# Three attentions of a transformer kernel: units of three heads taken in pairs

## The reference, cut to what matters

```python
# first: head size 64, values 16 wide per head, positional scores added
content_score = einsum('bind,bjnd->bnij', q + r_w_bias * SCALE, k)
attn_prob = softmax(content_score + rel_shift(pos_score), axis=-1)
attn_vec = einsum('bnij,bjnd->bind', attn_prob, v) @ Wo + bo
# second: head size 16, values 16 wide
# third:  head size 64, values 64 wide
scores = einsum('bqhd,bkhd->bhqk', q, k) * scale
out = einsum('bhqk,bkhd->bqhd', softmax(scores, axis=-1), v) @ Wproj
```

## Time and profile before

| | us |
|---|---|
| runs | 1655.21, 1665.26, 1647.38 (median 1655.21) |
| the profiled execution | 1649.25 |
| its span, first to last instruction | 1647.5 |
| PE busy / PEld / DVE / ACT / POOL | 1426.8 / 1050.3 / 684.2 / 664.3 / 387.5 |
| score matmuls L1928, 1152 records, busy | 140.8 |
| transposes L1967 / values L1957, busy | 92.7 / 85.9 |
| exponentials L1619 and accumulator reads, busy | 332.1 |
| key copies L1764 (48) and L1792, L1793 (48), busy | 28.4 and 24.2 |

### The profile page before, as it was taken

The page is one execution under the profiler, slowest core; times in us unless marked ns, Lnnn a source line. Parts: engine busy times, 40 slices in busy tenths (PEclk is TensorE's granted clock), DMA queues, the critical chain, the costliest instruction groups (busy, mean ns, idle before and its releaser), DMA issues.

```text
span 1647.5 us, 31617 instructions
## 1 busy us (share of the span) xinstructions
PE 1426.8 (87%) x10268; PEld 1050.3 (64%) x10268; DVE 684.2 (42%) x2126; ACT 664.3 (40%) x2241; POOL 387.5 (24%) x468
## 2 busy tenths in 40 slices
PE   5899897788779678888998998799999999989994
PEld 3556665643334456666678898376676776879993
DVE  5567766611112765444326322344343323451113
ACT  1668665320001337777531122265455442213331
POOL 5213212300000232222101565122121100024441
PEclk9899997578877799999999899799999999889997
DMA  7433432649997000000005664200000300135553
GB/s 224 125 100 103 115 90 56 235 161 418 419 417 226 5 0 1 0 0 0 0 0 144 184 198 123 61 2 0 0 0 0 134 0 0 41 118 183 184 164 106
DMA packets 94439, 178.73 MB, mean 108 GB/s; under 512 B 35578, under 2 KB 54168, under 8 KB 92704
## 3 DMA queue, kind: packets, MB, share of 16 engines
q1 hardware_dynamic: 80144, 130.65, 25.2%
q10 hardware_dynamic: 7056, 30.67, 4.5%
q0 software_dynamic: 7136, 16.10, 3.2%
HBM read 150.39 MB, written 26.99 MB: 108 GB/s over the span
## 4 chain that ended last, share of the span: by engine, by line
PE 61%; issue 12%; DVE 12%; ACT 6%; DMA 6%; SPq 2%; POOL 1%; DVEq 0%; ACTq 0%; POOLq 0%
PE bank L1837 15%; PE bank L2357 6%; PE bank L2343 5%; PE bank L1928 4%; DMA AREA<-in_fc 4%; PE bank L1940 4%; PE bank L1957 3%; PE bank L2347 3%; PE bank L1967 3%; PE bank L2018 2%; PE bank L1903 2%; ACT ON L1619 2%; PE bank L2010 2%; PE bank L2274 1%; DVE MXU L929 1%
## 5 line engine op out<-in xcount | busy, mean ns | idle before, releaser
L1837 PE MATMUL bank<-XT,AREA 96*128 96x408 f32 (+1 forms) x640 | 239.4, 532 | 33.1 <-ACT XT L1573 15.7
L1837 PEld LDWEIGHTS bank<-XT,AREA 96*128 96x128 f32 (+1 forms) x640 | 121.9, 196 | 139.7 <-issue 100.1
L1928 PE MATMUL bank<-KZ,QT 128*102 128x102 f32 x1152 | 140.8, 262 | 9.0 <-ACT PB L1619 5.8
L666 POOL TENSOR_TENSOR PB<-PB,RCU 102x306 f32<-102x306 f32 x96 | 69.2, 720 | 317.0 <-DVE RCU L935 316.9
L650 POOL TENSOR_TENSOR RS<-VE,expo 102x4 f32<-102x4 f32 (+1 forms) x53 | 53.0, 1000 | 376.0 <-DVE VE L875 326.3
L1928 PEld LDWEIGHTS bank<-KZ,QT 128*102 128x102 f32 x1152 | 122.4, 174 | 27.2 <-issue 18.2
L2357 PE MATMUL bank<-WM,KZ 128*128 x660 | 118.2, 327 | 0.0
L2357 PEld LDWEIGHTS bank<-WM,KZ 128*128 128x128 f32 x660 | 105.7, 190 | 0.4
L1600 ACT ACTIVATE KZ<-bank,AREA 128x128 f32<-128x128 f32 x198 | 54.8, 375 | 121.7 <-PE bank L2347 121.7
L1940 PE MATMUL bank<-AREA,OT 128*102 128x192 f32 x384 | 88.9, 345 | 11.3 <-DVE SLOTS L1291 5.2
L1957 PE MATMUL bank<-PT,V 102*32 102x102 f32 (+1 forms) x1152 | 85.9, 270 | 14.5 <-DVE OT L945 12.3
(11 more groups left out here) (335 smaller groups left out, 2734.3 us busy)
## 6 DMA issues: line engine op xcount, KB each, us to landing
AREA<-in_fc SPq DMA_DIRECT2D x10, 1536.0 KB, 21.5
SLOTS<-in_m3w SPq DMA_DIRECT2D x33, 384.0 KB
WM<-in_fc ACTq DMA_DIRECT2D x5, 2304.0 KB, 14.5
WM<-in_fc SPq DMA_DIRECT2D x6, 1536.0 KB, 21.2
AREA<-in_fc ACTq DMA_DIRECT2D x4, 2304.0 KB, 15.2
SLOTS<-in_m1w SPq DMA_DIRECT2D x33, 256.0 KB
AREA<-pos_scratch SPq DMA_DIRECT2D x16, 459.0 KB
pos_scratch<-AREA SPq DMA_DIRECT2D x8, 913.5 KB
```

Of the source, the lines that this page charges most:

```text
L666: pool.tensor_tensor(p, p, scale, ALU.mult).then_inc(sem["probs_ready"], 1)
L1837: last = pe.matmul(dst, lhsT, rhs, start=n == 0, stop=n == len(pieces) - 1)
L1928: last = pe.matmul(psum[k][0:T, cols(j)], QT[:, tile, cols(bb)], KALL[:, unit % per_tile * (HEADS // per_tile) + tile, cols(bb)], start=Tr ...
```

## The change

Attention goes in **pairs** of units, `(2p, 2p + 1)`, which belong to one sample. `KT` holds the keys once, without zeros, written by one instruction for a tile; the zeros and their semaphore `halves_cleared` go. A score matmul contracts only the rows of its head (64, or 32 of which 16 are used), and the six score matmuls of a pair alternate between its two units, that is between two row ranges and two banks. On PE, step `p` is now: values of pair `p - 3`, transposes of pair `p - 2`, `pos(2p)`, scores of pair `p`, `pos(2p + 1)`, part of a projection; an attention has 12 steps. Without `pos` the scores have four banks, with it two; values have bank 4 alone. On ACT `pos(s)` comes before the exponentials of `s`; the rest of its order stays.

```diff
-        SCORES, VALUES = (SBANKS + XBANKS[:1], SBANKS), (OBANKS[:1] + XBANKS[1:], OBANKS[:1])
+        PAIRS = UNITS // 2
+        PAIR_STEPS = PAIRS + 4
+        SCORES, VALUES = (SBANKS + XBANKS, SBANKS), OBANKS[0]
...
-            return min(UPB * bb + UPB + 6 + i, STEPS - 1)
+            return min(UPB // 2 * (bb + 1) + 3 + i, PAIR_STEPS - 1)
...
-            pool.memset(KZ[:], 0.0).then_inc(sem["halves_cleared"], at.one("halves_cleared"))
-            pool.wait_ge(sem["halves_cleared"], at.now("halves_cleared"))
...
             def attention(dv, pos, finish, between=None):
-                for s in range(STEPS + 1):
-                    n = s - 6
-                    if 0 <= n < UNITS and av_filled(dv, n % UPB):
+                for s in range(2 * PAIR_STEPS):
+                    n = s - 5
+                    if s % 2 == 0 and 0 <= n < UNITS and av_filled(dv, n % UPB):
...
-                ts(KZ[0:64, 0, p, :], src[0:64], bk0[0:64, p:p + 1], None, ALU.add)
-                free(ts(KZ[64:128, 1, p, :], src[64:128], bk0[64:128, p:p + 1], None, ALU.add), k)
+                free(ts(KT[:, p, :], src, bk0[:, p:p + 1], None, ALU.add), k)
...
                         free(activation(PT[s % 2][:, 0:HPU, :], src, ACT.Copy), k)
+                    if pos:
+                        pos(s)
                     if s < UNITS:
...
                         give(last, "exp_ready")
-                    if pos:
-                        pos(s)
...
-                    src = full(k)[:, 0:TG]
-                    for u in range(UPB):
-                        rows = slice(32 * u, 32 * u + 32)
-                        last = activation(KALL[rows, 3 * u + j, :], src[rows], ACT.Identity,
-                                          bias=bqk1[rows, 3 + j:4 + j])
-                    free(last, k)
+                    free(activation(KT[:, j, :], full(k)[:, 0:TG], ACT.Identity, bias=bqk1[:, 3 + j:4 + j]), k)
...
+                def values(pair):
+                    f = fill_of(dv, pair[0])
+                    if pair[0] == 0:
+                        moved(*v_moved)
+                    moved(pt_moved[pair[0]], pt_moved[pair[1]])
+                    if f >= 1 and (pair[0] % UPB == 0 or av_filled(dv, pair[0] % UPB - 1)):
+                        taken(f - 1)
+                    for n in pair:
+                        for j in range(HPU):
...
+                def scores(pair):
+                    bb, dk = pair[0] // UPB, 128 // per_tile
+                    for n in pair:
+                        k = banks[n % len(banks)]
+                        if n < len(banks):
+                            pe.wait_ge(sem[f"bank_free{k}"], at.now(f"bank_full{k}") + 1)
+                        else:
+                            pe.wait_ge(sem[scores_read], at.take(scores_read))
+                    for j in range(HPU):
+                        for n in pair:
+                            rows = slice(n % per_tile * dk, n % per_tile * dk + dk)
+                            tile = n % UPB // per_tile * HPU + j
+                            last = pe.matmul(psum[banks[n % len(banks)]][0:T, cols(j)], QT[rows, tile, cols(bb)],
+                                             KT[rows, tile, cols(bb)], start=True, stop=True)
...
+                for step in range(PAIR_STEPS):
+                    pair_of = lambda n: (2 * n, 2 * n + 1) if 0 <= n < PAIRS else None
+                    if pair_of(step - 3):
+                        values(pair_of(step - 3))
+                    if pair_of(step - 2):
+                        turn(pair_of(step - 2))
+                    if pos:
+                        pos(2 * step)
+                    if pair_of(step):
+                        scores(pair_of(step))
+                    if pos:
+                        pos(2 * step + 1)
+                    project_values(step)
```

More of the change, by code:

```diff
@@ L675, in _ @@
             powers(1)
-            pool.wait_ge(sem["power_out"], at.now("power_out"))
-            for half in range(2):
-                pool.memset(KZ[64 - 64 * half:128 - 64 * half, half, :, :], 0.0
-                            ).then_inc(sem["halves_cleared"], at.one("halves_cleared"))
-            pool.wait_ge(sem["halves_cleared"], at.now("halves_cleared"))
             words(NB // 2, NB, "words_behind")
@@ new lines, in project_values @@
+                def project_values(step):
+                    for bb in range(GB):
+                        for i in range(2):
+                            if step != proj_step(bb, i):
+                                continue
+                            if i == 0:
+                                taken(fills(dv) * (bb + 1) - 1)
+                                claim(None, PROJBANK)
+                            half = (parts + 1) // 2
+                            for m in (range(half), range(half, parts))[i]:
+                                last = pe.matmul(psum[PROJBANK][0:T, 0:D], OT[bb % 2][:, m, :], wo[:, m, :],
+                                                 start=m == 0, stop=m == parts - 1)
+                            if i == 1:
+                                filled(last, PROJBANK)
@@ L2004, in _ @@
             moved(*r_moved[-2:])
-            pe.wait_ge(sem["halves_cleared"], at.take("halves_cleared", 2))
             def project(w, p6):
```

85 lines of the change are left out of this document (16 added, 69 removed).

## The result

The changed kernel takes 1764.68 us (median of 4 runs, 1754.69 to 1768.46) against 1657.7 us for the kernel before beside it: ratio 1.064, 95% interval 1.058 to 1.070. The profiled execution took 1754.69 us, forecast 1755.

A forecast was written before the change was run, and what follows sets the result against it. TensorE, busy 87% of the span, was taken to bound the kernel. 1649.25 - 7.8 - 7.2 + 23.6 + 10.6 = 1668 at full clock, plus 87 for the clock: 1755 profiled, 1760 forecast, range 1662 to 1795.

The forecast's parts named there:

- The loop: Second and third attention: each step waits for ScalarE's copy behind the newest exponentials; 4.02 and 4.20 us a pair, +23.6 and +10.6 us.
- The bare sum of 1668: Whole kernel at full clock: 1649.25 us less 7.8 and 7.2 saved, plus 23.6 and 10.6 for the closed loop.
- Scores: TensorE, a pair's twelve score records by turns on two row ranges: 0.74 us, where two units took 1.08.
- Entry: TensorE, time ahead of a pair's scores for getting into the row-range mode: 0.09 us.
- Zeros: Row normalisations on VectorE no longer slowed by memsets on GpSimd: 4.0 + 3.8 = 7.8 us saved; third memset costs nothing.
- key copies: Ahead of the second attention TensorE waits 1.13 and 0.67 us behind twelve key copies; three remain, 7.2 us saved.
- First attention: Loop there too, but ScalarE frees positional banks earlier: 0 at full clock, bounds -2 to +3 us a group.
- The clock: TensorE falls to 1.2 GHz at group starts, loop gaps keep it low: +47 second, +24 third, +16 first attention, 87 us.
- The faster rival: Copies of transposes not waited for; ScalarE paces second attention at 2.82 us, TensorE third at 3.13; about 1638 us, chance 0.14.

## Why the prediction was right, and where it was not

The sum, against the profiled execution before, by stretches that the first scores of each attention bound:

| | predicted | measured |
|---|---|---|
| up to the second attention's first scores | -7.8 - 1.8 + 16 = +6.4 | 637.3 to 639.0: +1.7 |
| from there to the third's first scores | 23.6 + 47 - 5.4 = +65.2 | 435.8 to 499.5: +63.7 |
| from there to the end | 10.6 + 24 = +34.6 | 574.4 to 614.5: +40.1 |
| sum | +106.2 | +105.5 |

That the sum came within 1 us is in part luck: the stretches are off by -4.7, -1.5 and +5.5 and cancel.

- **The loop: right and shown.** Two edits that break it on different engines give back 78 and 79 us. Its sum of rows was exact: 4.00 and 4.20 us with the clock held, 5.45 to 5.54 and 5.91 at the low clock (forecast 5.52 and 5.9). What stands around the turns was reckoned too short. With the clock held the scores of pair 2 began at 5.03 us (0.45 + 4.58), not 4.85 (the terms given for it add up to 4.78), and those of pair 3 at 9.8 us (4.73 later), not 8.9; the added matmuls may have a part in this. From the scores of the third attention's last pair to the next group's first it took 40.7 us, where 62.7 - 34.3 + 11.1 = 39.5 was reckoned. So the 2.65 us a group for the loop at full clock in the third attention was too low. The bare sum of 1668 was not run; the kernel with added matmuls bounds it by 1727 from above.
- **Scores: right.** At full clock a pair's twelve records last 0.79 us and the next instruction starts 0.72 after the first of them (660.02 to 660.74 in the kernel with added matmuls); forecast 0.74. Entry, 0.09, shows in the transposes ahead: 0.66 instead of 0.58. The price of the switch that the earlier trace rows gave holds. By the 4 ns of the Trainium skill's TensorE: Matmul & The Clock Gate (Part 3, measured speedup against the span model) a pair was estimated at 0.55; the trace does not agree, with 0.72.
- **Zeros: right** for both memsets, 5.04 to 1.40 and 5.24 to 1.25, 7.6 of 7.8 us. The key copies' two waits ahead of the second attention are gone. Ahead of the first attention more was saved than the 3.8 us reckoned: its first scores began at 56.2 us instead of 62.6, 6.4 earlier. TensorE waits for key copies there too, 0.61 and 0.74 us before the change and 0.68 once after it, a place that I had left out.
- **First attention: the groups right, the reason half wrong.** In the second and third group the scores of pairs 3, 5 and 7 and the next group's came at 15.8, 32.5, 44.0 and 61.4 us; stepping gave 15.5, 30, 41.6 and 57.6 at full clock, and 61.6 with two low pairs. But I counted ScalarE's earlier emptying of the positional banks as a gain that pays for the loop. Alone it costs 13 us (0.8%). It is not a gain but a condition: without it pairs cost 90 us more. Against the kernel before the three periods between groups are 7.1, 3.5 and 3.4 us longer, 14.0 together, where I had 0 and, for the clock in four groups, 16; the whole stretch lost only 1.7, since more was saved ahead of its scores.
- **The clock: its size not shown, its cause wrong in part.** Of the 87 us that I gave it the runs show at least 34: a group of the second attention lost at least 58.0 - 50.5 = 7.5 us to it (forecast 11.8), one of the third at least 0.8 to 2.4 (forecast 6). How much of the rest was the clock and how much the loop is not known. I put the fall down to a group's idle start and its staying down to gaps in the loop, 80% busy as in the long low stretch of the earlier trace rows. But it stayed down at 99% busy with the loop gone, at 96% without any loop, and fell at steady pairs with the starts filled; with whole rows it came back at 70% busy. The scores on a part of the rows keep it down: putting them in (keys once, old order) and taking them out (whole rows, with the loop and without) move it each time. Gaps matter beside them: with whole rows and the loop it still falls for 10.2 to 13.7 us a group, and added matmuls over all rows hold it at 1.00. In the third attention it came back in mid-group, as forecast, once the projections filled the wait. Whether the unused rows or the changes between row ranges do it is open; no run separates them. And not every stage with matmuls on a part of the rows is held down: in the second expert layer of the kernel before, 396 of 1265 records are on halves of the rows, by turns, at 1.00 for 157 us:

```profile
1469.40:1626.40 157.00, 151.42 (x1265) 142.43 (x1264) 25.88 (x99) 54.78 (x198) 64.95 (x65) 1.00 0.55 167
```

- **The faster rival had its numbers right** (pairs at 2.80, forecast 2.82; third attention 2.81 to 3.43 around 3.13) and its condition: the copies must pass the exponentials. With that, and with the clock held by added matmuls, the change pays: 0.988.

## What to carry to other kernels

Before work is taken in larger bundles, write down for each engine what stands in front of the instruction that the next bundle waits for: one copy behind the newest exponentials turned a stream into a round trip over four engines, and its period can be added up from rows of the old trace. Take matmuls on a part of the rows as a risk for the clock, and read the granted clock beside the busy share: TensorE can be busy 99% at 0.50, and one short whole-row matmul in each gap can be worth more than it costs, though not in a stage that holds the clock without it. Check a forecast that came true by stretches too, since errors in two terms can cancel. Try the parts of a change both alone and undone, since a part can lose 13 us by itself and save 90 with the others.

## What the runs showed of the hardware

- TensorE stayed at 1.2 GHz for 51.2 us with its records filling 49.28 of them, and for 30.7 us at 30.31, both with scores on 32 rows; with whole rows it returned to 2.4 GHz after 6.8 us at 4.73. The busy time of the records is not all that the clock follows. Nor is it enough that some matmuls use half of the rows: 157 us with 396 such records of 1265 stayed at 2.4 GHz.
- Scores of successive units on different row ranges overlap without being issued by turns. At the start of a group in the kernel with keys once and the old order, three units of six records last 1.31 us together, where before they took 1.83:

```profile
645.78 1.31 PE L1905 MATMUL bank<-KZ,QT 32*102 32x102 f32 x18
```
